# Unread bf16 products on TensorE at its waits in the routing of a two-layer mixture and attention kernel

## The reference, cut to what matters

```python
logits = x @ W_router                      # x normalized, 4096 x 4
expert_idx = jnp.argmax(logits, axis=-1)
h = gelu(jnp.einsum('th,ehi->tei', x, W1) + b1)       # 4 experts, 256 -> 1024
intermediate = jnp.einsum('te,tei->ti', onehot(expert_idx), h)
y = layer_norm(intermediate @ Wo + bo + x) * gamma + beta
x = x + 0.5 * y
```

## Time and profile before

| what | value |
|---|---|
| median of 3 runs | 2108.85 us (2106.52 to 2109.03) |
| profiled execution, own time | 2111.9 us |
| its span in the trace | 2110.2 us |
| PE busy | 2011.4 us, 95% of the span |
| DVE busy | 1480.5 us, 70% |
| ACT busy | 987.2 us, 47% |
| POOL busy | 927.7 us, 44% |

### The profile page before, as it was taken

How to read it: one execution, slowest core, us unless ns; L and a number is a source line. 1 busy time by engine, 2 the same in 40 slices (tenths; PEclk the granted TensorE clock), 3 DMA queues, 4 the chain that set the end, 5 groups by cost and what they waited for, 6 DMA issues and landing times.

```text
span 2110.2 us, 41681 instructions
## 1 busy us (share of the span) xinstructions
PE 2011.4 (95%) x13717; PEld 1403.2 (66%) x13717; DVE 1480.5 (70%) x4068; ACT 987.2 (47%) x2304; POOL 927.7 (44%) x1139
## 2 busy tenths in 40 slices
PE   6999999889999999987999998999999999899998
PEld 5999996534444444446899995776666666567776
DVE  6433555388888888724457747999877777698884
ACT  2333333326666666652333443333347777534332
POOL 5423655421111112113342456555656767465553
PEclk9999999969999999997999999999999999999999
DMA  6556753555334543113365663000000000000000
GB/s 199 196 194 215 241 198 118 164 66 62 49 44 61 62 57 47 22 42 113 123 207 196 216 231 74 1 0 0 1 1 2 2 2 2 2 11 13 16 20 20
DMA packets 101711, 173.59 MB, mean 82 GB/s; under 512 B 14704, under 2 KB 66320, under 8 KB 101520
## 3 DMA queue, kind: packets, MB, share of 16 engines
q1 hardware_dynamic: 95376, 154.40, 28.2%
q0 software_dynamic: 6144, 16.79, 2.4%
HBM read 136.01 MB, written 34.87 MB: 81 GB/s over the span
## 4 chain that ended last, share of the span: by engine, by line
PE 38%; DVE 11%; issue 5%; ACT 1%; POOL 0%; DVEq 0%; SPq 0%; DMA 0%; ACTq 0%; POOLq 0%
PE s_Y L1887 5%; PE s_HH L793 5%; PE s_Y L805 5%; PE s_R L1857 4%; PE s_HH L1857 4%; PE s_HH L2211 3%; PE s_R L2198 2%; PE s_R L2232 1%; PE s_R L1879 1%; PE s_R L2246 1%; PE s_Y L2282 1%; PE s_Y L2290 1%; DVE s_HH L1750 1%; DVE ff_hscale L1570 1%; DVE fw_down L1573 1%
## 5 line engine op out<-in xcount | busy, mean ns | idle before, releaser
L1465 DVE TENSOR_REDUCE a_part_max<-a_psS 128x1 f32<-128x512 f32 (+3 forms) x608 | 362.7, 655 | 76.0 <-PE a_psS L1393 67.5
L1521 ACT ACTIVATE a_PT<-a_psE 128x512 f32<-128x512 f32 (+1 forms) x608 | 309.2, 583 | 175.8 <-PE a_psE L1409 158.9
L1368 POOL TENSOR_SCALAR_AFFINE_SELECT a_PT<-a_PT 128x512 f32<-128x512 f32 x128 | 81.6, 637 | 398.6 <-ACT a_PT L1521 398.6
L1800 POOL TENSOR_TENSOR fw_down<-fw_down,ff_hm 128x704 f32<-128x704 f32 x64 | 97.5, 1524 | 226.0 <-DVE fw_down L1582 226.0
L1822 ACT ACTIVATE ff_hm<-fw_down 128x704 bf16<-128x704 f32 x64 | 50.6, 790 | 286.6 <-DVE fw_down L1573 286.6
L1887 PE MATMUL s_Y<-w_down,fw_up 128*128 128x256 f32 x768 | 177.9, 382 | 3.9 <-DVE X L1767 3.0
L1857 PE MATMUL s_R<-w_gate,ff_xqT 128*128 128x512 f32 (+1 forms) x512 | 165.7, 467 | 10.0 <-ACT ff_sil L1832 10.0
L1857 PE MATMUL s_HH<-w_up,ff_xqT 128*128 128x512 f32 (+1 forms) x512 | 162.7, 461 | 2.1 <-DVE fw_down L1573 2.1
L1887 PEld LDWEIGHTS s_Y<-w_down,fw_up 128*128 128x128 f32 x768 | 144.8, 191 | 21.3 <-issue 3.2
L1425 PE MATMUL a_psO<-a_PT,a_va 128*32 128x512 f32 (+3 forms) x1536 | 150.4, 494 | 2.5 <-POOL a_PT L1368 1.8
L1387 PE MATMUL a_psS<-a_sk,a_sq 96*128 96x512 bf16 (+2 forms) x480 | 143.7, 334 | 1.9 <-DVE a_part_max L1465 0.3
(11 more groups left out here) (486 smaller groups left out, 4288.2 us busy)
## 6 DMA issues: line engine op xcount, KB each, us to landing
e_w<-w_in SPq DMA_DIRECT2D x70, 1024.0 KB
e_xs<-sorted_x SPq DMA_DIRECT2D x70, 128.0 KB
e_xr<-sorted_x SPq DMA_DIRECT2D x70, 128.0 KB
sorted_y<-e_yo SPq DMA_DIRECT2D x70, 128.0 KB
a_sq<-qk_parts SPq DMA_DIRECT2D x60, 128.0 KB, 6.3
a_sk<-qk_parts SPq DMA_DIRECT2D x60, 128.0 KB, 6.9
sq<-qk_parts SPq DMA_DIRECT2D x36, 128.0 KB, 5.9
sk<-qk_parts SPq DMA_DIRECT2D x36, 128.0 KB, 6.4
```

Source lines behind the costliest of these rows:

```text
L1368: pool.affine_select(out=hidden, in_=hidden, compare_op=ALU.is_ge, fill=0.0, base=0, pattern=[[0, HG], [1, P]], channel_multiplier=-1).the ...
L1465: dve.tensor_reduce(part_max[:, c, h0:h0 + heads, qt], psS[place % RING][:, 0:heads * n].rearrange("p (h k) -> p h k", h=heads), AX.X, ALU ...
L1521: act.activation(PT[kt % 2][:, h0:h0 + heads, q0:q0 + n], psE[e % RING][:, 0:heads * n].rearrange("p (h q) -> p h q", h=heads), ACT.Exp, s ...
L1800: c.link(pool.tensor_tensor(hv[i], hv[i], hm[i][:], ALU.subtract))
```

## The change

A helper `keep_up(pe, n)` writes n products of the bf16 identity with itself, repeated four times, 512 columns wide, into the bank `T` (`psIdle`), which nothing reads until slot 0's tokens are turned into it. It is called at six places, each directly ahead of a wait: two products in `router` of the eight tiles before `FIRST_TILES`, six in `count_up` of the group that completes the first tiles, two in `add_up`, five in `position`, three in `list_slots`, and sixteen in slot 0's `turn`. That is 48 products in each of the two routings, 96 in all. Nothing is removed, and no wait is added.

```diff
+    def keep_up(pe, n):
+        wide = st.ident_bf[:].unsqueeze(1).broadcast_to([P, 4, P])
+        for _ in range(n):
+            pe.matmul(psIdle.rearrange("p (a q) -> p a q", q=P), st.ident_bf[:], wide, start=True, stop=True,
+                      skip_group_check=True)
...
         def router(t, p):
+            if FIRST_TILES - 2 * G <= t < FIRST_TILES:
+                keep_up(pe, 2)
             pe.wait_ge(evacuated, t + 1)
...
         def count_up(t, p):
             g = t // G
+            if t + G == FIRST_TILES:
+                keep_up(pe, 6)
             pe.wait_ge(choice, CHOICE * (g + 1))
...
         def add_up(t, p):
+            keep_up(pe, 2)
             pe.wait_ge(table1, COUNTS1)
...
         def position(t, p):
+            keep_up(pe, 5)
             pe.wait_ge(table1, FILLED)
...
         def list_slots(t, p):
+            keep_up(pe, 3)
             pe.wait_ge(table1, MARKED1)
...
     def tensor(pe):          # in experts()
         def turn(t, p):
+            if t == 0:
+                r.keep_up(pe, 16)
             pe.wait_ge(x_in[p], 8 * (t - p) + 16)
```

More of the change, by code:

```diff
@@ L254, in make_tables, with route @@
     c.end()
-def route(nc, st, sem, tag, ctx, plan, psT, psY, psA, psL, psFirst, area=None):
+def route(nc, st, sem, tag, ctx, plan, psT, psY, psA, psL, psFirst, psIdle, area=None):
     names = ("yturned yevac projected joined moment rooted normed turned evacuated logit choice ranked placed masked "
@@ L690, in route @@
     parts.first_tiles, parts.first_slots = FIRST_TILES, FIRST_TILES - EXPERTS + 1
+    parts.keep_up = keep_up
     parts.halved = (halved, 3) if not after_attention else None
@@ L1188, in first_layer_phase @@
         st.gathered = ctx.enter_context(nc.sbuf_tensor("b_gathered", [P, RING, D], F32))
-        r = route(nc, st, sem, "r0_", ctx, Plan(first_tiles=12, delay=0, steps=4, hop=3), RT, RY, RA, RL, Y)
+        r = route(nc, st, sem, "r0_", ctx, Plan(first_tiles=12, delay=0, steps=4, hop=3), RT, RY, RA, RL, Y, T[:])
         e, gather, ends = experts(nc, st, sem, "e0_", ctx, r, T, [H0, H1], Y, ring=RING)
@@ L2340, in second_layer_phase @@
         r = route(nc, st, sem, "r1_", ctx, Plan(first_tiles=16, delay=16, steps=3, hop=2), half(R0, 0), half(R0, 1), half(R1, 0),
-                  half(R1, 1), Y, work.sil)
+                  half(R1, 1), Y, T[:], work.sil)
         e, gather, ends = experts(nc, st, sem, "e1_", ctx, r, T, [half(HH, 0), half(HH, 1)], Y, fp4=st.fp4)
```

## The result

| what | before | after |
|---|---|---|
| median of 6 runs each, side by side | 2108.94 us (2106.28 to 2109.72) | 2121.18 us (2114.52 to 2121.63) |
| ratio after / before | | 1.0056 [1.0042, 1.0070] |
| profiled execution, own time | 2111.9 us | 2121.61 us |
| its span | 2110.2 us | 2119.9 us |

The change makes the kernel slower by 0.56%, 12.2 us by the medians. The prediction, 2104.4 us, had the wrong sign, and the result lies 10 us above its range. The two profiled executions differ by 9.7 us in span; the one of before lay 3 us above its median.

A forecast was written before the change was run, and what follows sets the result against it. PE, busy 95% of the span, was taken to bound the kernel. First mixture 1.0 - 3.7 = -2.7 us and second -1.7 us gave -4.4 us: 2104.4 us from the 2108.85 us median, range 2099.5 to 2111.0 us.

The forecast's parts named there:

- The step that failed: First routing's router: clock rises after one or two more pairs, DVE slips 1.2 us, bounds 0.9 to 2.6 us.
- The rises within 3.7 to 4.6 us: Slot 0 and 930.35 us: clock rose 4.6 and 3.7 us into wide products, taken as evidence that pairs raise it.
- the 55%: 934 to 956 us: clock stays up with L456 products filling 55% of the time, compared with about 40% for pairs.
- booked the sixteen at nothing: Ahead of slot 0's tokens: sixteen take 3.5 to 5.7 us, covered by PE's wait; cost 0 to 0.4, taken 0.
- Rival C: PE, 19 to 34 us: routing products stay slow to the end; +6.1 us in all, 2115.0 us; chance 0.13.
- Behind the tokens: First mixture after slot 0's tokens: full-speed PE work gains 3.7 us, bounds 1.9 to 5.2 us.
- rival B: First mixture: late rise, pairs cost 2.6 us, late weights cut gain to 1.9 us; -1.2 us, 2107.7 us; chance 0.28.
- One for one: Slots, PE nearly always busy from 80 to 300 us: moving their beginning moves the end by as much.
- The second mixture: Sixteen in PE's 3.94 us wait keep the clock up; 4.7 us become 3.0 us: -1.7 us, bounds 0 and -4.
- The reading of the clock: First routing: durations show 1.2 GHz until about 59.5 us, although the granted-clock column says 1.00; durations decide.

The follow-up runs named there:

- a2: After with only the pairs in the router of eight tiles kept, no table products and no sixteen: 2116.62 us, ratio to before 1.0039.
- a4: After plus twelve more products at the very start of the first routing: 2119.36 us, ratio to before 1.0051.
- b2: After with four products instead of two in each of the eight router steps: 2118.27 us, ratio to before 1.0026.
- a1: After with only the sixteen products ahead of slot 0's tokens kept, in both routings: 2106.26 us, ratio to before 0.9991.
- b1: a1 plus eight products ahead of slot 1's tokens in the first mixture: 2107.61 us, ratio to before 0.9981.
- b4: After without the pairs in the router steps; table products and the sixteen stay: 2111.66 us, ratio to before 1.0001.
- c2: b1 plus six products ahead of tile 28's transposes in the first mixture: 2108.16 us, ratio to before 0.9983.
- c3: c1 and c2 together: 2107.96 us, ratio to before 0.9980.
- c1: b1 with ten instead of sixteen products ahead of slot 0's tokens in the first mixture: 2108.23 us, ratio to before 0.9986.
- a3: After with only the table's products kept (six, two, five, three): 2110.67 us, ratio to before 1.0012.
- b3: After with twelve products at the start, pairs in twelve tiles of each routing, none in the table, sixteen kept: 2114.48 us, ratio to before 1.0011.

## Why the prediction was wrong, point by point

**The step that failed** is this one: "I expect the rise after one or two more pairs. DVE then slips by 1.2 us." No pair raised the clock: 0.86 us of products in every 2.0 to 2.6 us stayed at half speed through all eight (after, a2, a4), and even 1.7 us in 2.9 us needed 15 us (b2). In place of 1.2 us, the pairs cost 5.0 us on the way to the table (a2), and the table's first count came 7.5 us later, where the forecast had DVE slip by 1.2 us. The rises within 3.7 to 4.6 us that I leaned on were in stretches of dense products, and the 55% was a stretch where the clock was already up. What holds a clock need not raise it: a2's second mixture held with what the first did not raise.

**Where the 11.6 us at slot 0's tokens come from.** PE's chain gives it without a rest. First count +7.5 us (pairs 5.0, six 2.5). From the count to `list_slots` 9.6 us instead of 7.0 us: +2.6 us, since the two, the five and the three ran slow too, with DVE waiting 1.71 us at `add_up`. From there to the sixteen 4.6 us instead of 4.7 us. Then 5.95 us of sixteen in place of a 4.35 us wait: +1.6 us. 7.5 + 2.6 - 0.1 + 1.6 = 11.6 us. From the transfer's side it is the same sum: SP issued the tokens' load at 53.96 us instead of 46.39 us, +7.6 us, and from its issue to the turned tokens it took 6.1 us instead of 2.1 us, +4.0 us. The forecast had booked the sixteen at nothing since a wait covers them. That cover had shrunk: the products ahead had delayed PE by 10.0 us at that place (54.09 us; before, its wait began at 48.47 - 4.35 = 44.12 us) and the tokens' load by only 7.6 us, which leaves some 2.0 us of the 4.35 us, and the sixteen took 5.95 us, where it had 3.5 to 5.7 us: 5.95 - 2.0 = 4.0 us.

**Rival C** had the place (PE from 19 to 34 us), the mechanism and the terms at the front: pairs 6.0 us (5.0), six 2.6 us (2.5). Its sum for the first mixture was 9.5 - 3.7 = +5.8 us. Slot 3's tokens show +7.5 us and the entry of the second mixture +8.3 us: it took the sixteen and the last calls of the table as still covered. For the second mixture it had +0.3 us, measured +1.1 us. So it was 3.3 us too small between profiles (6.1 against 9.4 us); most of the rest of the 12.2 us is that the profiled execution of before was itself 3 us above its median, that of after only 0.4 us.

**Behind the tokens** the forecast was right for after and wrong for the idea. In after, slot 3's tokens come 24.4 us behind slot 0's against 28.5 us: 4.1 us, forecast 3.7 us. But there the tokens were late: SP issued slot 1's tokens and slot 0's weights some 7.8 us later than before (56.40 and 55.23 us, against 48.63 and 47.46 us) and PE came 11.6 us later, so it waited for neither. In a1, with the tokens on time, 1.5 us were left of it; rival B's 1.9 us is the nearer number, with slot 1's tokens as the late party rather than the weights. "One for one" held to 0.8 us: 7.5 us at slot 3 are 8.3 us at the second mixture's entry.

**The second mixture** was forecast at -1.7 us. The stretch behind its tokens is fast as said (L463 1.03 us at 995.15 us; the 0.50 stretch is gone), and b1, with POOL's gap as in before, shows the 1.7 us. In after it is +1.1 us, since pairs and six, slow from 967 us on, hold up the scatters; rival C had +0.3 us net.

**The reading of the clock** by durations instead of the column held in every kernel. The Trainium skill, "TensorE: Matmul & The Clock Gate", section "Seeing it yourself", calls the gate's trace events unreliable; the column here bears that out: it is 1.00 over half-speed stretches until the first change that it records, and agrees with the durations behind one (a4).

**What stays open.** POOL's wait of about 2.5 us ahead of a scatter of the second mixture stands in the profiles of before, after (2.95 us at 978.74 us), a4, b1 to b4, c2 and c3, in c1 with 1.83 us, and not in a1, a2 and a3; no edit goes with it, and I found nothing that ends it. By one pair of profiles it is worth 1.7 us: a1 and b1 have the same second mixture, and slot 0's tokens come 53.84 us behind its entry in a1, without the wait, and 55.52 us in b1, with it. So a1's profile, 5.8 us shorter than that of before, flatters the sixteen. And the fours of b2, the pairs of a2 and b3 give runs some 6 us apart; that they differ in where the clock rises or falls is inferred from the profiles' differences between kernels and from the mean granted clocks of b3's runs, not shown by two profiles of one kernel.

## What to carry to other kernels

Products that are to raise the clock belong in one dense block, in a wait that is longer than the block's length at half speed; count them all at half speed until a trace shows them faster, and ask first what runs ahead of that wait and could eat its cover. Thin filler on a chain without slack cost nearly its full half-speed length here (5.0 us for seven uncovered pairs of 0.86 us) and raised nothing. And ask what the raised clock would gain there: where another engine sets the pace, as DVE in this routing, it is nothing.

## What the runs showed of the hardware that I had not expected

- The same thin work can hold a clock that is up, though it did not raise one that was down: a pair of 512-column bf16 products per tile (0.43 us in 0.8 to 1.6 us, once in 2.7 us) stayed fast in b3's first mixture and in a2's second; 0.86 us in 2.0 to 2.6 us stayed slow for 15 us in after and a2. In the second mixture of after and a4 the clock fell all the same, at the second pair.
- Where a dense block raises the clock varies between executions of the same instructions from the same start: sixteen from 43.96 us took until 48.64 us in a1 and until 49.98 us in b1, with the same work ahead of them. Six in a row raised it in a3 and b4 (from 31.7 us) and not in after and a4 (from 36.7 us). The fall varies too: in the same wait for ACT's copy PE lost the clock in b1 (1.68 us) and kept it in c1 (1.69 us).
- Four tiles of transposes and 4-column router products without a filler lost a clock that twelve products had raised (a4, between 13.6 and 14.7 us), with waits of 0.22 to 0.58 us between them. The Trainium skill, "TensorE: Matmul & The Clock Gate", Part 4, says that a transpose in transpose mode does not count as PE-busy the same way; this fits, but does not tell the transposes from the waits.
